# A vision-tower block on one core: elementwise products and low parts moved from VectorE to GpSimd, five unread products added, all order lists written anew

## What is computed

```
h = patches(x) @ tok_W.T;  h = concat([cls_tok, h])
h = h + attn(layernorm(h))
h = h + ffn(layernorm(h))

attn(x):  h = ln(x);  k, v = h @ Wk.T, h @ Wv.T;  sr = sigmoid(h @ Wr.T)
          y = bi_wkv(decay / T, first / T, k, v);  x = x + (sr * y) @ Wo.T
          h = ln(x);  x = x + sigmoid(h @ Wr_f.T) * (square(relu(h @ Wk_f.T)) @ Wv_f.T)
bi_wkv:   af, bf, mf (forward scan) and ab, bb, mb (backward scan) of
            mm = max(m + w, k);  a = exp(m+w-mm) * a + exp(k-mm) * v;  b = ... + exp(k-mm)
          kk = k + u;  M = max(mf, mb, kk);  ef, eb, ec = exp(mf-M), exp(mb-M), exp(kk-M)
          y = (ef*af + eb*ab + ec*v) / (ef*bf + eb*bb + ec)
ffn(x):   16 sigmoid scores, 2 of 4 groups, then 4 experts, weights normed to 2.5
          sum of silu(x @ Wg) * (x @ Wu) @ Wd over the chosen experts and one shared expert
```

## Time and profile before

| | us |
|---|---|
| median of 3 runs | 255.41 (255.34 to 255.53) |
| the profiled execution | 255.63 |
| its span, first to last instruction | 253.5 |
| TensorE busy in the span | 242.6 (96%) |
| VectorE busy | 191.4 (76%) |
| ScalarE busy | 151.0 (60%) |
| GpSimd busy | 17.9 (7%) |

### The profile page before, as it was taken

The page is one execution under the profiler, slowest core; times in us unless marked ns, Lnnn a source line. Parts: engine busy times, 40 slices in busy tenths (PEclk is TensorE's granted clock), DMA queues, the critical chain, the costliest instruction groups (busy, mean ns, idle before and its releaser), DMA issues.

```text
span 253.5 us, 4370 instructions
## 1 busy us (share of the span) xinstructions
PE 242.6 (96%) x1508; PEld 222.6 (88%) x1508; DVE 191.4 (76%) x490; ACT 151.0 (60%) x311; POOL 17.9 (7%) x29
## 2 busy tenths in 40 slices
...
GB/s 170 332 176 309 85 243 62 38 0 0 0 3 10 106 94 13 0 3 0 1 11 157 185 43 1 1 3 0 82 173 136 18 3 0 1 40 92 102 33 27
DMA packets 13165, 17.46 MB, mean 69 GB/s; under 512 B 2359, under 2 KB 11224, under 8 KB 13016
## 3 DMA queue, kind: packets, MB, share of 16 engines
...
## 4 chain that ended last, share of the span: by engine, by line
PE 73%; ACT 9%; DVE 8%; issue 4%; DMA 3%; SPq 2%; POOL 0%; DVEq 0%; POOLq 0%
PE PA L998 16%; PE PG L978 16%; PE PG L980 11%; PE PF L998 7%; PE PQ L978 4%; PE PQ L980 3%; PE PX L1029 2%; DMA gates<-c_rows 2%; PE PQ L1049 2%; PE PF L988 1%; PE PG L1149 1%; PE PG L1148 1%; DMA gates<-in_w_k 1%; ACT norm L422 1%; PE PF L1013 1%
## 5 line engine op out<-in xcount | busy, mean ns | idle before, releaser
L584 ACT ACTIVATE act<-PG,columns 128x222 f32<-128x222 f32 (+3 forms) x56 | 28.4, 507 | 58.8 <-PE PG L980 55.1
L978 PE MATMUL PG<-stack,hi_egu 128*128 128x222 f32 (+1 forms) x288 | 62.2, 324 | 0.0
L927 DVE SCALAR_TENSOR_TENSOR hid<-PG,columns,act 128x222 f32<-128x222 f32 (+1 forms) x52 | 27.3, 524 | 28.3 <-PE PG L980 24.8
L998 PE MATMUL PA<-w_ed,hid 128*124 128x192 f32 (+1 forms) x240 | 46.3, 328 | 0.4 <-DVE hid L936 0.3
L978 PEld LDWEIGHTS PG<-stack,hi_egu 128*128 128x128 f32 x288 | 45.6, 190 | 0.7 <-DVE hid L927 0.2
L980 PE MATMUL PG<-stack,lo_egu 128*128 128x222 f32 (+1 forms) x192 | 42.7, 304 | 0.0
L998 PEld LDWEIGHTS PA<-w_ed,hid 128*124 128x124 f32 (+1 forms) x240 | 38.5, 183 | 1.2 <-DVE hid L936 1.2
L980 PEld LDWEIGHTS PG<-stack,lo_egu 128*128 128x128 f32 x192 | 31.8, 190 | 0.0
L396 POOL TENSOR_TENSOR rstd<-var,minus_half 112x2 f32<-112x2 f32 (+3 forms) x12 | 13.9, 1156 | 186.8 <-DVE var L671 186.8
L936 DVE TENSOR_TENSOR hid<-hid,gates 128x222 f32<-128x222 f32 (+1 forms) x48 | 21.9, 462 | 1.8 <-DMA gates<-c_rows 0.9
L998 PE MATMUL PF<-w_down,mix_hid 128*124 128x192 f32 (+1 forms) x120 | 22.8, 326 | 0.0
...
## 6 DMA issues: line engine op xcount, KB each, us to landing
gates<-in_w_egu SPq DMA_DIRECT2D x6, 512.0 KB, 4.8
...
```

The source lines that it names most:

```text
L584: nc.scalar.activation(act[128 - gate:128, n % 2, 0:G.n], PG[0:gate, gate_bank(n), 0:G.n], ACT.Silu, bias=bias).then_inc(act_silu, 1)
L927: V_.scalar_tensor_tensor(out, PG[part, 1, 0:G.n], bias, act[part, i, 0:G.n], ALU.add, ALU.mult).then_inc(mul_done, 1)
L978: mm(out, w_hi[:, slot, cols], x[:, p, 0:G.n], start=(p == 0), stop=False, skip_group_check=True)
L998: last = mm(tile_out(P, G, t), src[:, G.ts[t]:G.ts[t] + G.tp], w, start=start and t != 1, stop=stop, skip_group_check=True)
```

## The change

- **Low parts.** For the pieces `rf`, `up0`, `up1` and `sgu` GpSimd takes the low part (`low_parts`); `split` counts them in a semaphore of their own, `pool_low`.
- **Own product, tail products, row sum.** GpSimd computes own (signal `pool_own`, waited for by sum2), the two tail products Zt (they wait for `tail_ready`, given by the tail's reciprocal, which now comes first; TensorE's o waits for `zt_ready` as well as `z_ready`) and base (`base_ready`). Norm 2 now waits for `x1_out` alone; h1 and the steps that write `h0` or `x1` anew wait for `base_ready`.
- **Unread products.** Three more behind H:tok (idle0 to idle2), one behind F0:kt and one behind F0:rt.
- **Lists.** All four are new; GpSimd's has 35 steps in place of 12 roots.

The diff, cut:

```diff
+POOL_LOW = ("rf", "up0", "up1", "sgu")
...
-            engine.wait_ge(lo_done, own)
+            by_pool = sum(p[0] in POOL_LOW for p in PIECES[:own])
+            engine.wait_ge(lo_done, own - by_pool)
+            if by_pool:
+                engine.wait_ge(pool_low, by_pool)
...
-            for n, g in POOL_ORDER:
-                root(n, g, 2 if n == 1 else 1)
+            def low_parts(pool):
+                for name in POOL_LOW:
...
+                    pool.wait_ge(hi_done, n + 1)
+                    nc.gpsimd.tensor_tensor(lo[name][:, :, :], src, hi[name][:, :, :].bitcast(F32), ALU.subtract).then_inc(pool_low, 1)
+                    yield name
+
+            def recurrence(pool, g):
+                G, wk = GROUP[g], GROUP[g].wk
+                pool.wait_ge(exp_out, at(exp_out, g, 5))
+                pool.wait_ge(act_kvr, at(act_kvr, g, 4))
+                nc.gpsimd.tensor_tensor(mx[:, OWN_V:OWN_V + wk], V[:, 0:wk], mx[:, OWN:OWN + wk], ALU.mult).then_inc(pool_own, 1)
+                yield "own"
+                pool.wait_ge(tail_ready, at(tail_ready, g, 1))
...
+                nc.gpsimd.tensor_tensor(zt[0:64, 0:G.half], K[0:64, G.blocks[1]], E1[0:64, tail], ALU.mult).then_inc(zt_ready, 1)
+                pool.wait_ge(zt_ready, at(zt_ready, g, 1))
+                nc.gpsimd.tensor_tensor(zt[64:128, G.half:G.n], K[64:128, G.blocks[1]], E1[64:128, tail], ALU.mult).then_inc(zt_ready, 1)
+                pool.wait_ge(zt_ready, at(zt_ready, g, 2))
+                yield "zt"
+                pool.wait_ge(x1_out, at(x1_out, g, 2))
+                if g >= 2:
+                    pool.wait_ge(norm_ready[3], at(norm_ready[3], g - 2, 1))
...
+                nc.gpsimd.tensor_tensor(base[g % 2][rs], h0[g % 2][rs], x1[rs], ALU.add).then_inc(base_ready, 1)
+                yield "base"
...
             since(act_e, z_ready, g)
+            since(act_e, zt_ready, g)
...
             since(act_e, norm_ready[2], g)
+            since(act_e, base_ready, g)
...
-            for h, s in enumerate(G.blocks):
-                step(V_.reciprocal(K[:, s], K[:, s]))
-                yield f"recip{h}"
+            V_.reciprocal(K[:, G.blocks[1]], K[:, G.blocks[1]]).then_inc(tail_ready, 1)
+            yield "recip1"
+            step(V_.reciprocal(K[:, G.blocks[0]], K[:, G.blocks[0]]))
+            yield "recip0"
...
-            v.wait_ge(x1_ready, at(x1_ready, g, 1))
+            v.wait_ge(x1_out, at(x1_out, g, 2))
...
+            v.wait_ge(base_ready, at(base_ready, g, 1))
             step(V_.scalar_tensor_tensor(h[rs], gate_r[rs], 0.5, base[g % 2][rs], ALU.mult, ALU.add))
...
+            for n in range(3):
+                spin()
+                yield f"idle{n}"
...
+            for after in ("kt", "rt"):
+                spin()
+                yield after
...
             pe.wait_ge(z_ready, at(z_ready, g, 1))
+            pe.wait_ge(zt_ready, at(zt_ready, g, 2))
...
-POOL_ORDER = [(1, 0), (1, 1), (2, 0), (1, 2), (3, 0), (2, 1), (1, 3), (3, 1), (2, 2), (3, 2), (2, 3), (3, 3)]
+POOL_ORDER = _order(
+    "R0:ln1 W:rf W:up0 R1:ln1 W:up1 F0:own F0:zt W:sgu R0:ln2 F0:base F1:own R2:ln1 F1:zt R0:ln3 F1:base R1:ln2 R3:ln1",
```

More of the change, by code:

```diff
@@ L256, in build @@
         z_ready = counted("z_ready", 1)
+        tail_ready, zt_ready = counted("tail_ready", 1), counted("zt_ready", 2)
+        pool_own = counted("pool_own", 1)
         pe_o = counted("pe_o", 2)
         x1_out = counted("x1_out", 2)
-        x1_ready = counted("x1_ready", 1)
+        base_ready = counted("base_ready", 1)
         front_step = [sem(f"front_step{g}") for g in range(len(GROUP))]
@@ L397, in root, with roots @@
                                         minus_half[0:G.tp, 0:cols, 0:G.tiles], ALU.pow).then_inc(pool_rstd[n], 1)
-            for n, g in POOL_ORDER:
-                root(n, g, 2 if n == 1 else 1)
+            def roots(pool, g):
+                for n, cols in ((1, 2), (2, 1), (3, 1)):
+                    root(n, g, cols)
+                    yield f"ln{n}"
+            def low_parts(pool):
+                for name in POOL_LOW:
+                    n, slots, cols = PIECE_AT[name], *PIECES[PIECE_AT[name]][2:4]
+                    src = raw[n % RING][:, 0:slots * cols].rearrange("p (s c) -> p s c", s=slots)
+                    pool.wait_ge(hi_done, n + 1)
[8 more added lines that the diff above has]
+                pool.wait_ge(tail_ready, at(tail_ready, g, 1))
+                since(pool, pe_o, g)
+                tail = slice(WK + G.n, WK + wk)
+                zt = Zt[G.n]
+                nc.gpsimd.tensor_tensor(zt[0:64, 0:G.half], K[0:64, G.blocks[1]], E1[0:64, tail], ALU.mult).then_inc(zt_ready, 1)
[6 more added lines that the diff above has]
+                    pool.wait_ge(norm_ready[3], at(norm_ready[3], g - 2, 1))
+                rs = (slice(0, G.tp), slice(0, G.tiles))
+                nc.gpsimd.tensor_tensor(base[g % 2][rs], h0[g % 2][rs], x1[rs], ALU.add).then_inc(base_ready, 1)
+                yield "base"
+            advance(tracks_of(pool, low_parts, R=roots, F=recurrence), POOL_ORDER)
         def act_high_parts(act_e):
@@ L761, in dve_front @@
                 yield f"weigh{d}"
-            v.wait_ge(exp_out, at(exp_out, g, 5))
-            step(V_.tensor_tensor(mx[:, OWN_V:OWN_V + wk], V[:, 0:wk], mx[:, OWN:OWN + wk], ALU.mult))
-            yield "own"
             settle()
@@ L794, in dve_front @@
                 yield f"x1{bank}"
-            v.wait_ge(x1_out, at(x1_out, g, 2))
-            rs = (slice(0, G.tp), slice(0, G.tiles))
-            V_.tensor_tensor(base[g % 2][rs], h0[g % 2][rs], x1[rs], ALU.add).then_inc(x1_ready, 1)
-            yield "x1"
         def edge_e1(wk):
```

17 lines of the change are left out of this document (9 added, 8 removed), and 114 rows, old and new, of tables (ACT_ORDER, DVE_ORDER, PE_ORDER).

## The result

The changed kernel takes 262.74 us (median of 4 runs, 262.48 to 263.36) against 255.43 of the kernel before: a ratio of 1.0287, 95% interval 1.0268 to 1.0305. It is 7.3 us slower, where 1.6 us less was forecast. The profiled execution took 262.48, its span 260.7. (GpSimd's new list has 28 steps, not the 35 named under the change: 12 roots, 4 low parts, and 4 each of own products, tail products and row sums.)

The account below looks back on a forecast made before the run. VectorE was taken to time group 0's output product, its gifts worth no more than TensorE's 4.2 us of holes. Terms + 0.8 - 0.66 - 0.7 = - 0.6, with half the conflicts - 1.6: 253.8 us, range 251.9 to 256.9.

Parts of the forecast that it names:

- Without any conflict: Rival for the whole kernel: GpSimd doesn't hold VectorE, terms together - 4.0 us, 251.4 to 252.2; chance 0.16.
- VectorE therefore times F0:o0: Group 0's output product on TensorE starts at 34.32 because VectorE's tail product ends at 34.30.
- The price: A GpSimd product was taken as two passes, 1.85 ns a column, 1.42 us for 768 columns.
- Both engines wait: Shared memory: GpSimd waits for two-tensor VectorE instructions, and by choice VectorE was taken to wait for GpSimd too.
- I take half: Only half of the 1.42 and 0.62 us of conflicts was counted, turning - 0.6 into - 1.6 us.
- Term 1: Up to group 0's output product: + 0.8 us; - 1.6 without conflict, + 2.7 at 2.77 ns a column.
- F1's k four microseconds ahead: Sign that the forecast is right: TensorE starts group 1's k some 4 us ahead of 35.58.
- Term 2: TensorE's hole at 45.27, a wait for ScalarE's copy, closes: - 0.66 us, or 0 if ScalarE is later.
- Term 3: From 56 to 90 us: - 0.7 us from the shift, tail products and own product, row sums taken as even.
- The unread products: Five added on TensorE to keep the clock up: put at 0, up to + 0.5, down to the 1.3.
- Nothing for the lists behind 90: Behind 90 us the new lists were given no effect; holes there would make the forecast wrong at its root.
- Slower, the port: Rival: every conflict paid at 2.3 ns a column, + 1.2 us, 256.6; decides from about 2.0 ns; chance 0.26.

Follow-up runs that it names:

- c1: The changed kernel with GpSimd's moved work left out, constants in its place; new lists and unread products remain: 256.36 us (+ 0.7).
- c2: The kernel before, on its own lists, with the same moved work left out of VectorE: 254.26 us (- 1.4).
- d3: c1 with the tail products and the row sums alone computed again, on GpSimd: 258.15 us (+ 2.6).
- a1: The changed kernel without its five added unread products, all else the same: 262.73 us (+ 7.1).
- e1: The changed kernel's lists and unread products, with every product, low part and row sum back on VectorE: 261.76 us (+ 6.4).

## Why the prediction was wrong, step by step

- **The error by size.** Forecast and result lie 8.9 us apart (- 1.6 against + 7.3), and two steps of the sum failed by about as much. Without any conflict the prediction had - 4.0 for terms 1 to 3; c1, the new lists and unread products without GpSimd's work, gives + 0.7, which is 4.7 off. For the conflicts the forecast then counted 2.4; GpSimd's work costs 6.6, which is 4.2 off. c1 in the three stretches:

```profile
16.00:44.00 28.00, 25.34 (x117) 18.05 (x115) 25.01 (x50) 25.43 (x56) 4.00 (x9) 1.00 0.56 189
44.00:66.00 22.00, 21.69 (x119) 16.23 (x120) 18.59 (x34) 18.06 (x39) 3.30 (x5) 1.00 0.05 11
66.00:90.00 24.00, 23.25 (x155) 20.71 (x155) 22.48 (x65) 20.98 (x43) 0.95 (x2) 1.00 0.17 37
```

  TensorE idles 2.66, 0.31 and 0.75 us, 3.7 in all, where the kernel before idles 4.2. So of the holes that the three terms were to close, the lists closed 0.5 in sum, and 1.6 opened behind 90. In the changed kernel the idle times are 2.4, 1.4 and 1.2 us longer than in c1: GpSimd's work opens holes in every stretch, not only ahead of the output product of group 0, where the prediction followed it.
- **What bounds the kernel.** That VectorE's gifts are worth no more than TensorE's holes held: c2 gives 1.4 to 2.5, not 4.2. But "VectorE therefore times F0:o0" was only half true. VectorE, then TensorE in c2, where VectorE has no tail products to do:

```profile
33.64 0.39 DVE L798 TENSOR_TENSOR Zm<-K,E 128x222 f32<-128x222 f32 x1
```

```profile
34.31 0.79 PE L1055 MATMUL PA<-hi_egu,minus_ident 128*128 128x512 f32 x1
34.94 0.81 PE L1041 MATMUL PF<-w_o,Zm 128*112 128x192 f32 x4
```

  Zm is done at 34.03, and the output product (line 1041) starts at 34.94, behind TensorE's own half of an egu piece without a gap; the old list keeps TensorE busy until then. An end that meets a start within 0.02 us, as 34.30 and 34.32 did, doesn't say which of two things that end there is the bound.
- **The price.** Taken 1.42 for 768 columns, measured 1.80 to 1.84 undisturbed, inside the bounds 0.71 and 2.13.
- **Both engines wait.** This choice was right, and "I take half" of the conflicts, a discount of 1.0 us, failed. They are paid in full, wherever a two-tensor instruction or a TENSOR_SCALAR stands beside a product. Term 1, from the first scan to the end of Zm: without conflict predicted 15.8, measured 16.2 in c1; up1 predicted 1.42, measured 1.35; own 0.62, measured 0.59; sgu 0.33, measured 1.30. The last is the one mis-sized: GpSimd began sgu's part at 34.41, behind both tail products of 0.49 each, and so under the last 0.33 of the reciprocal, not under two thirds of it.
- **F1's k four microseconds ahead.** It came (31.98), and hardly anything of it was left at the next step. ScalarE's copy of it:

```profile
36.55 0.48 ACT L514 ACTIVATE K<-PG 128x370 f32<-128x370 f32 x1 [2.15 <-DVE Zm L825]
```

  It starts at 36.55, before at 36.77. It waits 2.15 us for Zm, since K holds group 0's reciprocals until then. That dependence wasn't in the working.
- **Term 2.** The hole at 45.27 went, and a wait for top (0.78 at 47.43) stands in its place.
- **Term 3.** Predicted - 0.7. With the tail products and row sums alone (d3) the time rises by 1.9. A routing instruction in d3, beside group 1's row sum on GpSimd from 72.74 to 74.16:

```profile
72.85 1.33 DVE L906 TENSOR_TENSOR group_score<-apart,beside_sum 112x8 f32<-112x8 f32 x1
```

  It takes 1.33 us in place of 0.17, in the changed kernel as well, where the row sums of groups 0 and 3 also make a shift last 0.96 each in place of 0.16. "I take the two as even" put the row sums at nothing, as if instructions that read little could not wait long; a held instruction waits for the rest of the product, however short it is itself.
- **The unread products.** Put at 0, up to + 0.5; alone they cost 1.8, in the changed kernel nothing that a1 could tell.
- **Nothing for the lists behind 90.** Wrong. At 210 VectorE's product waits behind M3's first steps, which wait for the store of group 1's rows. SyncE, VectorE's first step of M3, then TensorE:

```profile
188.33 13.56 SPq L349 DMA_DIRECT2D gates<-c_rows  x24
```

```profile
208.48 0.55 DVE L857 SCALAR_TENSOR_TENSOR gate_r<-gate_r,PF 112x384 f32<-112x384 f32 x1 [2.13 <-DMA out<-h]
```

```profile
210.78 1.24 PE L1034 MATMUL PA<-w_ed,hid 128*124 128x192 f32 x6 [1.35 <-DVE hid L972]
```

  SyncE issues that store (out<-h) behind 24 transfers of gates, which begin 9 us later than before (188.33 against 179.36). In c1 they begin 3.2 later (182.53): so much comes with the new lists, the rest is the delay that GpSimd's work has added by then. The hole is in c1 too (1.42) and small in e1 (0.20), so it came with the lists, and its size hangs on the rest.
- **The rivals.** "Slower, the port" was the mechanism, and 2.34 ns is past its point of 2.0. It gave 256.6, as it followed the conflicts hardly further than the output product of group 0 and kept the gains of the lists, which c1 doesn't show.

Where the 7.3 us come from, by the runs: the moved work taken away on the old lists - 1.4 (c2), the new lists and unread products + 2.1 (c1 less c2), the work on GpSimd + 6.6. The first two are differences to kernels that leave work out. The split hangs on the order in which the steps are taken: by way of e1 the new lists with the work still on VectorE cost 6.4, and moving it to GpSimd adds only 0.9. Shown is that GpSimd's work costs 6.6 on these lists against no work at all, and that VectorE's instructions carry it. How the 2.1 splits between the store, the unread products and the order wasn't tried, and why the same work costs so much more on the new lists than on the old ones stays open.

Without GpSimd's work (c1) the output product starts at 33.99 and group 1's subtractions at 44.09, 2.5 and 3.3 us ahead of the changed kernel, although c1's trace starts later (group 0's first norm at 10.81 against 10.05).
